# At most two gathers of node rows on their way, in a two-layer graph network kernel

## The reference, cut to what matters

```python
edge_index = jnp.stack([src, dst])
# layer 0: one gather of x by src, a weighted sum per dst, two dense layers
msg = edge_weight[:, None] * x[src]
agg = jax.ops.segment_sum(msg, dst, num_segments=N)
h = jax.nn.relu((x + agg) @ W1 + b1)
x = _layernorm(x + h @ W2 + b2)
# layer 1: three hops, each with a gather of all the rows agg[tail]
head, tail = edge_index[0], edge_index[1]
rel = edge_emb[edge_type]
for _ in range(3):
    left = agg[head] @ q_w
    right = jnp.tanh(rel * agg[tail] @ k_w)
    att = jnp.sum(left * right, axis=1)
    ...
    msg = w[:, None] * rel * agg[tail]      # w: softmax of att within a head
    agg = segment_sum(msg, head) / count, then scaled to length 1
    out = out + agg + entity_emb
```

## Time and profile before

| what | us |
|---|---|
| device time, median of 3 | 9158.42 |
| lowest, highest | 9154.59, 9167.25 |
| span of the profiled execution | 14895.7 |
| busy in it: PE / DVE / ACT / POOL | 9009.4 / 6224.1 / 6149.7 / 6417.6 |
| gathers on POOL (L621), busy in it | 4732.3 + 1585.1 |

### The profile page before, as it was taken

One profiled execution on the slowest core, in us unless ns is written; L12 is line 12 of the kernel. 1 busy time (PEld: TensorE's weight loads), 2 busy tenths in 40 slices (PEclk: granted clock), 3 DMA queues, 4 the chain that ended last, 5 costly groups with the idle time before them and its releaser, 6 DMA issues. The chain is left out here.

```text
span 14895.7 us, 251017 instructions
## 1 busy us (share of the span) xinstructions
PE 9009.4 (60%) x47197; PEld 6806.5 (46%) x47197; DVE 6224.1 (42%) x27880; ACT 6149.7 (41%) x15788; POOL 6417.6 (43%) x6756
## 2 busy tenths in 40 slices
PE   2465555566777777777755555555555556555665
PEld 2343443444555555555544444444444444444444
DVE  3555555565333333333343333333334333333334
ACT  1355555553333333333334444444443444444443
POOL 4554554442444434444334444444434444444443
PEclk7566666667777777777777777777777777777777
DMA  2111111112444444444433333333343333333333
GB/s 63 37 37 34 36 35 35 33 35 77 127 125 126 125 125 126 125 125 126 124 102 105 106 104 106 104 105 101 108 99 105 104 104 107 102 105 105 109 109 93
DMA packets 1390477, 1399.81 MB, mean 94 GB/s; under 512 B 239512, under 2 KB 1066681, under 8 KB 1390137
## 3 DMA queue, kind: packets, MB, share of 16 engines
q1 hardware_dynamic: 1173398, 951.42, 21.2%
q0 software_dynamic: 216064, 444.28, 12.3%
q10 hardware_dynamic: 876, 2.56, 0.1%
HBM read 888.87 MB, written 183.76 MB: 72 GB/s over the span
## 5 line engine op out<-in xcount | busy, mean ns | idle before, releaser
L621 POOL DMA_INDIRECT tails<-node_rows,idx x4992 | 4732.3, 948 | 6564.6 <-ACT idx L649 5017.2
L1753 DVE SCALAR_TENSOR_TENSOR acc<-acc,fade,banks 128x129 f32 x4992 | 1718.4, 344 | 5486.8 <-remote 3164.9
L1838 PE MATMUL banks<-rt,weight_t 128*128 128x129 f32 x9984 | 1783.3, 335 | 1486.3 <-issue 802.1
L1838 PEld LDWEIGHTS banks<-rt,weight_t 128*128 128x128 f32 x9984 | 1607.8, 244 | 1631.4 <-issue 1206.6
L621 POOL DMA_INDIRECT l_rows<-in_x_dram,l_idx x1664 | 1585.1, 953 | 1529.5 <-ACT l_idx L649 1017.3
L1846 ACT ACTIVATE weight_t<-banks 128x512 f32<-128x512 f32 x1248 | 745.5, 597 | 3569.1 <-remote 2286.4
L1825 PE MATMUL banks<-ident,weight 128*128 128x128 f32 x4992 | 1070.4, 353 | 1878.0 <-ACT weight L1866 1767.1
L1818 PE MATMUL banks<-right,window 128*128 128x128 f32 x9984 | 1774.8, 335 | 459.9 <-issue 459.2
L1818 PEld LDWEIGHTS banks<-right,window 128*128 128x128 f32 x9984 | 1590.2, 242 | 538.2 <-issue 510.7
L1829 PE MATMUL banks<-rtt,k_sb 128*128 128x512 f32 x2496 | 1741.3, 789 | 1.4 <-ACT rtt L1853 1.4
L1825 PEld LDWEIGHTS banks<-ident,weight 128*128 128x128 f32 x4992 | 752.0, 181 | 2041.5 <-ACT weight L1866 1931.4
(11 more groups left out here) (309 smaller groups left out, 9792.2 us busy)
## 6 DMA issues: line engine op xcount, KB each, us to landing
window<-qt SPq DMA_DIRECT2D x4992, 64.0 KB
rel<-rel_kept SPq DMA_DIRECT2D x832, 256.0 KB
rows_in<-tile_rows SPq DMA_DIRECT2D x416, 256.0 KB
rel_kept<-rel SPq DMA_DIRECT2D x416, 256.0 KB
mask<-mask_kept SPq DMA_DIRECT2D x832, 128.0 KB
tails<-node_rows,idx POOLq DMA_INDIRECT x4992
mask_kept<-mask SPq DMA_DIRECT2D x416, 128.0 KB
l_rows<-in_x_dram,l_idx POOLq DMA_INDIRECT x1664
```

Of the source, the lines that this page charges most:

```text
L621: e.indirect_dma_start(out=rows[:, g, t % GROUP, :], out_offset=None, in_=of, in_offset=bass.IndirectOffsetOnAxis(ap=idx[:, b, t:t + 1], a ...
L1753: e.scalar_tensor_tensor(to, to, fade[:, g2, t:t + 1], bank[b_acc + t // 2][:, t % 2 * WIDE:t % 2 * WIDE + WIDE], ALU.mult, ALU.add).then_ ...
L1838: mm = e.matmul(bank[b_acc + t // 2][:, t % 2 * WIDE:t % 2 * WIDE + WIDE], weight_t[:, s.slot(4, 2), t, :], rt[:, s.slot(4, UNROLL), t, :] ...
```

## The change

Two semaphores instead of four count the landings, one for even gathers, one for odd. Ahead of each gather POOL now waits until the gather two places ahead of it has landed. In the loop this is two waits for each gather, one against the constant 16 and one against a register `before_it`, which grows by 16 after every second gather; ahead of the loop it is one wait against a constant. The consumers now wait for both semaphores to have counted all gathers up to their group (`landed`). Gathers, their order, their destinations and the three waits ahead of a batch stay as they were.

```diff
+IN_FLIGHT = 2
...
-        sp_tail = [sem(f"sp_tail{i}") for i in range(RING)]
+        sp_tail = [sem(f"sp_tail{i}") for i in range(IN_FLIGHT)]
...
+        def landed(lag):
+            return [(s, done(lag, 16 * GROUP // IN_FLIGHT)) for s in sp_tail]
+
         def pool_rows(e, name, rows, idx, of, s_free):
-            def batch(b):
-                for t in range(BATCH * GROUP):
-                    g = b * BATCH + t // GROUP
-                    e.indirect_dma_start(out=rows[:, g, t % GROUP, :], out_offset=None, in_=of,
-                                         in_offset=bass.IndirectOffsetOnAxis(ap=idx[:, b, t:t + 1], axis=0)).then_inc(sp_tail[g].h, 16)
+            def gather(n, b):
+                t = n % (BATCH * GROUP)
+                e.indirect_dma_start(out=rows[:, b * BATCH + t // GROUP, t % GROUP, :], out_offset=None, in_=of,
+                                     in_offset=bass.IndirectOffsetOnAxis(ap=idx[:, b, t:t + 1], axis=0)).then_inc(sp_tail[n % IN_FLIGHT].h, 16)
             for b in range(2):
                 e.wait_ge(s_copy_idx.h, s_copy_idx.at(b + 1))
-                batch(b)
+                for n in range(b * BATCH * GROUP, (b + 1) * BATCH * GROUP):
+                    if n >= IN_FLIGHT:
+                        s = sp_tail[n % IN_FLIGHT]
+                        e.wait_ge(s.h, s.at(16 * (n // IN_FLIGHT)))
+                    gather(n, b)
...
+            e.reg_mov(before_it, sp_tail[0].at(16 * (2 * BATCH * GROUP // IN_FLIGHT)))
             with e.Fori(0, z.slot_groups // BATCH // 2 - 1):
                 for b in range(2):
                     e.wait_ge(s_free.h, s_free.at(BATCH))
                     e.wait_ge(s_free.h, freed)
                     e.wait_ge(s_copy_idx.h, copied)
-                    batch(b)
+                    for n in range(BATCH * GROUP):
+                        s = sp_tail[n % IN_FLIGHT]
+                        e.wait_ge(s.h, s.at(16))
+                        e.wait_ge(s.h, before_it)
+                        gather(n, b)
+                        if n % IN_FLIGHT == IN_FLIGHT - 1:
+                            e.reg_add(before_it, before_it, 16)
                     e.reg_add(freed, freed, BATCH)
                     e.reg_add(copied, copied, 1)
...
-                    s.wait_ge((sp_tail[g4], ring_count(1, RING, 16 * GROUP)), (s_acc, done(3)))
+                    s.wait_ge(*landed(1), (s_acc, done(3)))
...
-                        s.wait_ge(here, (sp_tail[g8], ring_count(1, RING, 16 * GROUP)), (s_acc, done(1 + UNROLL)))
+                        s.wait_ge(here, *landed(1), (s_acc, done(1 + UNROLL)))
```

More of the change, by code:

```diff
@@ L634, in pool_rows @@
                     e.wait_ge(s_copy_idx.h, copied)
-                    batch(b)
+                    for n in range(BATCH * GROUP):
[5 more added lines that the diff above has]
+                            e.reg_add(before_it, before_it, 16)
                     e.reg_add(freed, freed, BATCH)
                     e.reg_add(copied, copied, 1)
-            e.free_register(freed)
-            e.free_register(copied)
+            for r in (freed, copied, before_it):
+                e.free_register(r)
         def first_idx(e, others, idx):
@@ L1426, in _ @@
                     first_idx(e, others, idx)
-                    phases(e, "ga", scalar_l0, z.slot_groups, steps, (UNROLL, 16 * GROUP))
+                    phases(e, "ga", scalar_l0, z.slot_groups, steps, (UNROLL, 16 * GROUP // IN_FLIGHT * UNROLL))
                 @block.vector
@@ L1446, in gnn_two_layers @@
             for s in sp_tail:
-                s.base += 16 * z.slot_tiles // RING
+                s.base += 16 * z.slot_tiles // IN_FLIGHT
             turned = tensor(ctx, "l0_turned", [P, 2, BANK])
@@ L1972, in _ @@
                         vector_q(e)
-                        pipeline(e, f"hd{hop}", vector_hop, z.slot_groups, deep, (UNROLL, 2 * UNROLL, GROUP * UNROLL, 16 * GROUP, 32))
+                        pipeline(e, f"hd{hop}", vector_hop, z.slot_groups, deep, (UNROLL, 2 * UNROLL, GROUP * UNROLL, 16 * GROUP // IN_FLIGHT * UNROLL, 32))
                         vector_nodes(e)
```

3 lines of the change are left out of this document (2 added, 1 removed).

## The result

| kernel, first chip | device time, median us | lowest, highest |
|---|---|---|
| before | 9162.83 (4 runs) | 9154.59, 9172.63 |
| after | 12651.99 (4 runs) | 12640.62, 12659.68 |

The ratio is 1.3807, 95% interval 1.3787 to 1.3826: 3489 us slower. Slower was forecast, but 11,850 us, in a range that ended at 12,450.

What follows compares the result with a forecast made beforehand. POOL's gathers in a row were taken as the bound, 9110 of 9158 us. 9158 + 2316 (held waits) + 374 (contention) = 11,848, rounded to 11,850 us; range 10,450 to 12,450.

Steps and rivals of the forecast that it cites:

- The met waits: Satisfied waits ahead of POOL's gathers: two waits and half an addition for each gather cost nothing by themselves.
- quiet S: S, from gather n-2's end on POOL to gather n's start: landing 1.52 plus wake 0.77, 2.29 us without contention.
- The rival of 1.97 us: Shorter landing and wake at POOL's held gathers, as at the first put: 10,409 us, 10,783 with contention; chance 0.27.
- quiet step, all gathers: POOL's pace with held gathers, without contention: two take 3.24 us, one 1.62, for all 6656 gathers.
- contention in the hops: Other DMA traffic delays landings in the hops: 0.075 us for each of 4992 gathers, +374 us; bounds 0 to 1148.
- outside the phases, and unexplained: Time outside the four phases, where POOL has no gathers, 644 us, plus 48 us of the 9158 left unexplained.
- The held waits: POOL held until the gather two places ahead lands: 1.62 us a gather instead of 1.272, 6656 x 0.348 = +2316 us.
- I add a third of that: Hops: a third of the two put rows' 0.46 us difference, 0.15 us between gather n-2's end and gather n's start.
- The rival of more contention: In the hops the extra is 0.46 us and more: +1148 us instead of 374, 12,620 us; chance 0.09 for over 12,400.
- I take this for the profile's own slowness: POOL's 5017.2 us of pauses for ACT's index copy belong to the profile, mostly gone in the 9158 us.
- the profiled execution should grow far less: Whole profiled execution: 15,000 to 15,900 us after the change, from 14,895.7, as batches there stand 18.4 us apart.
- my rival of a gain: Window loads land sooner; the gathers' pace keeps time over 9110 us, so at most 48 us, 0.5%; chance 0.03.

Runs made afterwards that it cites:

- fly4: Changed kernel with four gathers allowed on their way instead of two, every wait instruction kept: 14,793 us, 1.0039 of the kernel before on the 2nd chip.
- fly1: Changed kernel with four semaphores, each gather waiting for the one just ahead (one on its way): 22,788 us, 1.5476 of the kernel before on the 2nd chip.
- after_small_loads: Changed kernel with the hops' window, relation and mask loads cut to one partition of 128: 12,168 us, 0.8281 of the kernel before on the 3rd chip.
- before_small_loads: Kernel before with the hops' window, relation and mask loads cut to one partition of 128: 14,613 us, 0.9935 of the kernel before, 3rd chip.

## Why the prediction was wrong

**The direction and its mechanism were right.** Every second gather is held, the releaser is the DMA two places ahead, gaps alternate, POOL's 948 ns stay, its wait for ACT's indices has gone, and consumers that now wait on two semaphores are late by POOL. The met waits cost POOL nothing, as said (fly4).

**The quiet S was right, term by term.** Foretold was 1.52 + 0.77 = 2.29 us. fly1 shows 1.52 to the last count and 0.76 from there to POOL's start, with nothing beside it, and the changed kernel 1.57 and 0.76 in layer 0. The row that the 1.52 was taken from holds as well: in the trace the last count comes 1.51 us behind the gather's end, and DVE starts 0.02 us later. The Trainium skill ("DMA: Bandwidth & Descriptors", "Anatomy of one DMA — SWDGE (gpsimd) path") gives such a DMA 2.0 us and its bytes over 436 GB/s, the update of its semaphore included, an estimated 2.15 us here; it doesn't say from which event. Counted from the instruction's start, as the prediction did, the trace has 0.94 + 1.52 = 2.46 us in fly1, 0.3 more, so the measurement decides. The rival of 1.97 us looked in the right place: a wait that the gather carries does wake sooner, at 1.81 to 1.83 us of S, but only gathers ahead of the loop have it in this kernel.

**The terms that were mis-sized.** The sum, by phases, against what was measured:

| term | foretold, us | measured, us | difference |
|---|---|---|---|
| quiet step, all gathers | 6656 x 1.620 = 10,783 | 6656 x 1.694 = 11,275 | +492 |
| contention in the hops | 4992 x 0.075 = 374 | 9227 - 4992 x 1.694 = 771 | +397 |
| outside the phases, and unexplained | 644 + 48 = 692 | 601 | -91 |
| sum | 11,849 | 12,647 | +798 |

(The third column's 9227 is the sum of the three hops, and 1.694 the mean step of layer 0. The split of 692 into 644 and 48 joins a trace of the slow pace with a time of the quick one.) The first term, the 6656 x 0.348 of *The held waits*, failed because one quiet row was taken for the mean. The median S of layer 0 gives (0.95 + 2.34) / 2 = 1.645 us; the mean of 2.44 gives 1.694. The times are skewed: one S in a hundred is under 2.21 us, and one in a hundred over 4.84. On average the count comes after 1.62 us instead of 1.52, and POOL starts after 0.82 instead of 0.77. The late starts are regular: about every 112th gather POOL starts 3.46 us after the last count, in all four phases, and the one behind it is late as well. The second failed in "I add a third of that": the hops have 0.31 us more of S than layer 0, not 0.15, nearly all of it in the counts (1.90 on average instead of 1.62), and after_small_loads, which takes it away in the second and third hop, shows that it is contention. The rival of more contention comes to 12,620 us, nearly the time measured, but by luck: its 0.46 us is half as much again as the hops have, and the rest was in the quiet step. The range ended at 12,450 because each term was given its typical row, and both errors had the same sign.

**The pauses in the profile were put aside too quickly.** "I take this for the profile's own slowness" was wrong: five chips take 14,692 to 14,913 us for the kernel before in their timed runs, and the same pauses are in the traces of its near variants there (POOL waits 4771.0 us for ACT's indices in before_small_loads). In every later run the profiled execution is within 1.1% of the median. The waits for "remote" were read wrongly too: they stand only for a releaser that the profile can't name, and they go with the slow pace (there in fly4, none in the changed kernel). And "the profiled execution should grow far less", to 15,000 at least, was wrong with it: it took 12,647. The 9158 us leave no room for those pauses, so the profiled execution of the earlier trace rows can't have run as the timed ones did; on which chip it ran isn't on record. On two of the other five, where it was timed, the same change is a gain of 14 and 15%, and my rival of a gain ended at 48 us, since I didn't ask what a slower POOL would give back to those it disturbs.

**What stays open.** That POOL's pace sets the 9163 us rests on arithmetic: gathers that nothing holds have a step of 1.25 us in every trace, 1.27 with their average gap. That makes 8320 to 8466 us, and with the 601 to 644 outside the phases 8921 to 9110, as a floor; the time is 0.6 to 2.7% above it. The changed kernel, whose time is its pace, fits. But the loss can't confirm it, since the time after would be the same whatever had set the time before. No trace or experiment on the kernel before exists from the first chip. PE, with 8617.0 us of busy time in the changed kernel at a mean granted clock of 0.78, may have been close behind.

## What to carry to other kernels

A limit on transfers in flight is priced at the mean time from one end to the next start, with the traffic of that stage, not at a quiet row: the late ones lie much further from the typical value than the early ones. A wait on which a queue is held again and again should be one that the waiting instruction carries itself; here that is 0.5 us of each S, as long as nothing else then holds the queue. And when a profiled execution is much longer than the timed runs, find out which of its waits grew and run the kernel on more chips before calling them the profile's: here they were the kernel's time on five chips of six.

## What the runs showed of the hardware that I had not expected

- The same kernel takes 9163 us in one place and 14,692 to 14,913 on five other chips, with the runs in one place within 1% of each other; the changed kernel takes 12,519 to 12,694 on three.
- While POOL issues gathers without a break, single register instructions of SP and DVE take 0.70 us instead of 0.04, more often the longer the row: 2% behind the first gather, 68% at the eighth for SP. In the changed kernel on the first chip none did.
- A separate wait instruction ahead of a gather delays its start by 0.5 us against a wait that the gather carries (0.76 and 0.26 us from the last count; S 2.34 and 1.81), and nothing if the wait is met (gap 0.30).
- About every 112th gather of the changed kernel, and every 110th of fly1, POOL starts 3.4 to 3.5 us after the last count instead of 0.76. The cause wasn't looked for.
- At the end of each phase, where the tiles are padding and their indices should all be the same, gathers come more slowly. The last gaps of the third hop in the changed kernel:

```profile
12560.81 0.94 POOL L625 DMA_INDIRECT tails<-node_rows,idx  x1 [2.43 <-DMA tails<-node_rows,idx]
12562.44 0.94 POOL L625 DMA_INDIRECT tails<-node_rows,idx  x1 [0.68 <-DMA tails<-node_rows,idx]
12565.10 0.94 POOL L625 DMA_INDIRECT tails<-node_rows,idx  x1 [1.72 <-DMA tails<-node_rows,idx]
```

The last thirty steps of a phase take 2.1 to 2.2 us on average instead of 1.7 to 1.9. It was seen in this place only; that the repeated index is the reason wasn't tested.
